# Latent attention: the maxima from bf16 parts in one matmul, over all steps, and the product one tile later

## What is computed

```
cq = x @ W_q                      # latent queries, 32 wide (4 copies on 128 partitions)
kh = maps[h].T @ keys             # keys of head h in the same 32 dimensions
tilt = keys . tilt[h]             # one number per key and head
s[k, q] = kh[:, k] . cq[:, q] + tilt[k]
p = exp(scale * (s - max_k s))    # scale = 1 / sqrt(128 + 32)
out[h] = (V.T @ p) / sum_k p      # V: 32 wide, the same for all heads
```

## Time and profile before

| what | value |
|---|---|
| median of 3 runs | 4385.51 us |
| the profiled execution | 4400.56 us |
| its span | 4398.8 us |
| granted clock, mean over the span | 0.90 |
| TensorE busy | 3628.2 us (82%) |
| VectorE busy | 3012.3 us (68%) |
| ScalarE busy | 2482.7 us (56%) |
| POOL busy | 1168.0 us (27%) |
| latent attention, head loop | 1095 to 1806 us of the span |

### The profile page before, as it was taken

How to read it: one execution, slowest core, us unless ns; L and a number is a source line. 1 busy time by engine, 2 the same in 40 slices (tenths; PEclk the granted TensorE clock), 3 DMA queues, 4 the chain that set the end, 5 groups by cost and what they waited for, 6 DMA issues and landing times. The chain is left out here.

```text
span 4398.8 us, 86825 instructions
## 1 busy us (share of the span) xinstructions
PE 3628.2 (82%) x33381; PEld 1655.7 (38%) x33381; DVE 3012.3 (68%) x4370; ACT 2482.7 (56%) x4824; POOL 1168.0 (27%) x1181
## 2 busy tenths in 40 slices
PE   5769998754888888687999997778995779999957
PEld 4523333633222222342222223355654612222237
DVE  6567774557565665658999994435994489999933
ACT  3436665463144444433888886434543548888844
POOL 2610000524465664000000000035883500000016
PEclk7879999876799999896999998878996879999979
DMA  3221110210000000002000000140001120000012
GB/s 122 70 78 38 40 42 15 83 32 9 2 4 5 7 4 5 18 0 71 27 25 31 31 21 3 27 116 14 1 1 63 57 76 25 31 31 23 20 54 73
DMA packets 82885, 153.20 MB, mean 35 GB/s; under 512 B 22940, under 2 KB 49196, under 8 KB 81580
## 3 DMA queue, kind: packets, MB, share of 16 engines
q1 hardware_dynamic: 56856, 105.74, 7.6%
q0 software_dynamic: 12704, 22.97, 1.8%
q10 hardware_dynamic: 12916, 18.93, 1.3%
HBM read 103.76 MB, written 31.20 MB: 31 GB/s over the span
## 5 line engine op out<-in xcount | busy, mean ns | idle before, releaser
L1516 DVE TENSOR_REDUCE 55_heads_mx<-55_heads_mps 128x1 f32<-128x1024 f32 x512 | 602.8, 1220 | 49.1 <-PE 55_heads_mps L1366 46.7
L1516 DVE TENSOR_REDUCE 32_heads_mx<-32_heads_mps 128x1 f32<-128x1024 f32 x512 | 602.7, 1220 | 47.5 <-PE 32_heads_mps L1366 45.1
L1486 ACT ACTIVATE 55_heads_p<-55_heads_sps 128x512 f32<-128x512 f32 x1024 | 553.7, 596 | 86.2 <-PE 55_heads_sps L1392 83.0
L1486 ACT ACTIVATE 32_heads_p<-32_heads_sps 128x512 f32<-128x512 f32 x1024 | 553.7, 596 | 85.9 <-PE 32_heads_sps L1392 82.5
L2581 ACT ACTIVATE 21_latent_heads_p<-21_latent_heads_ring 128x1024 f32<-128x1024 f32 x256 | 257.8, 1024 | 350.9 <-PE 21_latent_heads_ring L2486 348.5
L1516 DVE TENSOR_REDUCE 7_heads_mx<-7_heads_mps 128x1 f32<-128x1024 f32 (+7 forms) x384 | 333.8, 909 | 147.7 <-PE 7_heads_mps L1374 100.9
L1486 ACT ACTIVATE 7_heads_p<-7_heads_sps 128x512 f32<-128x512 f32 (+3 forms) x640 | 308.1, 533 | 156.2 <-PE 7_heads_sps L1395 116.5
L2610 DVE TENSOR_REDUCE 21_latent_heads_mx<-21_latent_heads_ring 128x1 f32<-128x1024 f32 x256 | 302.3, 1220 | 130.0 <-PE 21_latent_heads_ring L2465 130.0
L2395 POOL TENSOR_TENSOR 21_latent_heads_psum<-21_latent_heads_psum,21_latent_heads_p 128x1024 f32<-128x1024 f32 x140 | 328.4, 2349 | 85.8 <-ACT 21_latent_heads_p L2581 81.0
L1392 PE MATMUL 55_heads_sps<-51_head_rows_qs,51_head_rows_ks 123*32 123x512 bf16 x4096 | 314.3, 383 | 8.3 <-ACT 55_heads_p L1486 5.0
L1392 PE MATMUL 32_heads_sps<-30_head_rows_qs,30_head_rows_ks 123*32 123x512 bf16 x4096 | 314.1, 383 | 8.4 <-ACT 32_heads_p L1486 5.0
(11 more groups left out here) (1217 smaller groups left out, 6778.8 us busy)
## 6 DMA issues: line engine op xcount, KB each, us to landing
3_routed_experts<-in_L0f_experts SPq DMA_DIRECT2D x8, 514.0 KB
9_routed_experts<-in_L0f_experts SPq DMA_DIRECT2D x8, 514.0 KB, 6.5
50_routed_experts<-in_L3f_experts SPq DMA_DIRECT2D x8, 514.0 KB
57_routed_experts<-in_L3f_experts SPq DMA_DIRECT2D x8, 514.0 KB
38_hale_masks_qs<-scratch_q_parts SPq DMA_DIRECT2D x11, 288.0 KB
38_hale_masks_ks<-scratch_k_parts SPq DMA_DIRECT2D x33, 96.0 KB
yT<-scratch_results SPq DMA_DIRECT2D x12, 256.0 KB, 6.3
y<-scratch_results ACTq DMA_DIRECT2D x12, 256.0 KB, 6.6
```

What stands on the lines that cost most here:

```text
L1486: act.activation(pslot[x % PS][:, 0:CW - off], sps[e % SB][:, 0:CW - off], ACT.Exp, scale=SCALE / 2).then_inc(ex_done, 1)
L1516: dve.tensor_reduce(mx[h % 2][:, i, half:half + 1], mps[x % 2][:, 0:w], AX.X, ALU.max).then_inc(mx_taken, 1)
```

## The change

It does these things, all in the latent attention:

- The maxima are made from bf16 parts in a single matmul per bank: `rough_k` holds keys rounded to bf16 (96 rows), where the second 32 rows become the rest (keys minus rounded keys), and 3 rows of tilt; `rough_q` holds the rounded queries, where the third 32 rows become their rest, and 3 rows of ones. 99 rows are contracted: rounded times rounded, rest times rounded, rounded times rest, and tilt. Rounding is ScalarE's, the rest VectorE's (`rest_of_keys`), and keys are made two heads ahead.
- Maxima run six units ahead of the score passes, and one comes with each score pass, over all 32 passes of a head: `maxima_at`. Per key tile the order is two score passes, two maximum passes, then the product of the tile before.
- A score pass takes its row groups by its queries' chunk: the even pass of a tile uses rows 0 to 63, the odd one rows 64 to 127. The tilt is no longer in the side matmul; it is the bias of the exponential, a column of `tilt_bias`. The side matmul only subtracts the maximum (`minus`), and `q_side` is 512 wide, filled by 12 DMAs of 4 x 128 elements where it was 4 of 48 x 128.
- The denominators' matmuls move to pass 9 (5 in the last head), in the order column group by column group. ScalarE copies their result. The reciprocal is in four pieces, at passes 11 to 14.
- POOL adds passes 0 to 25, and in the last head the even ones up to 22; VectorE adds the rest, three passes late.

The core of the diff:

```diff
-    SUMS = 6
-    FIRST, LAST = 6, 24
-    TURNED = 28
-    MAKE = (FIRST - 1, FIRST + 1)
-    BY_DVE = tuple(range(24, S))
+    AHEAD = 6
+    SUMS = 9
+    MAKE = (17, 21)
+    TURNED = 29
+    LAG = 3
+    INVERT = (11, 12, 13, 14)
+    BY_DVE = tuple(range(26, S))
...
+        def maxima_at(h, p):
+
+            v = h * U + p + AHEAD
+            return [(1 + v // U, v % U)] if v < U * LASTH else []
...
                 for h in range(MLA_H):
                     sp.wait_ge(m_copied, h + 1)
-                    for top in range(0, P, DC):
-                        sp.dma_start(q_side[h % 2][top + 3:top + 6, :], mT[h % 2][0:PARTS, :]).then_inc(m_in[h % 2], 16)
+                    for c in range(NC):
+                        for a in range(3):
+                            at = a * NT + TPC * c
+                            sp.dma_start(q_side[h % 2][DC * c + a:DC * c + a + 1, :], mT[h % 2][at:at + TPC, :]).then_inc(m_in[h % 2], 16)
...
                     for x in range(2):
-                        r = rows(number, x)
-                        pe.matmul(bank(number, x), cq[r, tile(i)], kh[h % 2][r, chunk(2 * pair + x)], start=True, stop=False,
-                                  tile_position=(r.start, 0))
...
+                        ins = pe.matmul(bank(("max", h, u), x), rough_q[0:K_ROWS, tile(i)], rough_k[h % 2][0:K_ROWS, chunk(2 * pair + x)],
+                                        start=True, stop=True)
+                    ins.then_inc(mx_ready, 1)
...
                     for p in range(S):
-                        scores(p, h)
...
+                        scores(h, p)
+                        if p % 2:
+                            for unit in maxima_at(h, p - 1) + maxima_at(h, p):
+                                max_pair(*unit)
+                            if p > 1:
+                                product(h, p // 2 - 1)
+                            elif h:
+                                product(h - 1, NT - 1)
+                        if h + 2 < MLA_H and p in MAKE:
+                            make_keys(h + 2, MAKE.index(p))
+                        if h and p == sums_at(h):
                             denominators(h - 1)
...
+                        act.activation(slot(p, h)[:], pair_of(("score", h, p))[:], ACT.Exp, scale=MLA_SCALE,
+                                       bias=tilt_bias[:, h, p // 2:p // 2 + 1]).then_inc(ex_done, 1)
```

353 lines of the change are left out of this document (191 added, 162 removed).

## The result

The changed kernel takes 4422.0 us (median of 4 runs, 4418.17 to 4426.78), the kernel before 4385.2 (median of 4, one run more than the three shown ahead): a ratio of 1.0082, 95% interval 1.0066 to 1.0098. It is slower by 0.8%. The prediction was 4337 us, faster, with a range up to 4385: wrong in its sign and outside its range.

A forecast was written before the change was run, and what follows sets the result against it. TensorE and the chain through it were taken to set the pace. Head 0 -6.7, heads 1 to 6 -31.9, head 7 -15.1, start +4.4, end +0.5 gave -48.8 us from 4385.5: 4337 us, range 4285 to 4385.

The forecast's parts named there:

- Other engines fit under it: Main loop: VectorE's two reductions a tile and POOL's 55.9 us a head fit under the chain's 64.2 us a head.
- before head 0: Start of the head loop: fewer tilt DMAs save time, subtractions and twelve DMAs add it, +4.4 us together.
- head 7, to its last exponential's end: Last head: POOL takes even sums up to pass 22, a tile per 2.33 us; 43.3 us, was 58.4.
- tail: End of the last head: the reciprocal cut in pieces adds 0.5 us.
- The tile of 4.01: Main loop: scores, exponential with bias, release, second maximum and product chain to 4.01 us a key tile, 64.2 a head.
- The boundary: Between heads: TensorE waits for twelve SP issues and their landing, 5.5 us, 8.1 before the last head.
- Half clock behind the boundary: First tiles after a head's boundary stall: TensorE at half clock for 7 us of work, costing 2.6 us a head.
- Rival 3: Main loop: POOL's later start or slower additions make the tile longer than its chain; +28 us, 4365; chance 0.13.
- Rival 1: Between heads: issues of short pieces are far cheaper, so stall and half clock go; 52 us less, 4285; chance 0.14.
- Rival 2: First tiles of each head: half clock lasts 4.5 tiles, costing 11.0 us instead of 2.6; 4396; chance 0.12.
- Rival 4: Main loop: score passes no longer overlap or another ring wait makes a tile 4.4 us; +44, 4381; chance 0.05.
- The signs I had listed for "wrong": Heads under 72 or over 85 us apart, exponentials waiting for POOL, low clock over half a head, or the product waiting.

The follow-up runs named there:

- experiment 2: The changed kernel with the rows of maxima sent in four DMAs a head instead of twelve: 4379.53 us, ratio 0.9978 to the kernel before.
- experiment 3: The changed kernel with POOL's additions on 8 of 1024 columns, result not the network's: 4334.94 us, ratio 0.9886 to the kernel before.
- experiment 4: The changed kernel with two additions fewer a head on POOL (VectorE from pass 24 instead of 26): 4409.6 us, ratio 1.0059 to the kernel before.

## Why the prediction was wrong

**The step that failed** is the one sentence on the other engines: "Other engines fit under it: VectorE has two reductions a tile ..., POOL 24 additions a head, 2.33 each ..., 55.9." Both fit by busy time and neither fits beside the other. The sum took VectorE's other instructions at the durations they have while POOL pauses and had no term for VectorE waiting for POOL. It also compared POOL's 55.9 us with the whole head, 64.2, though POOL's share lies in passes 2 to 25, twelve tiles of 4.01, which are 48.1. At a turn of 4.11 us POOL needs 4.6 for its two additions, falls behind, and makes 12 or more additions without a pause before the multiplication comes. That made the multiplication 9.5 us, the stall behind it 5.74, and a second stretch at half clock. It cost 8 us in head 0, 9 to 13 in each of heads 1 to 6, and 4 to 7 us in and behind the last head. With most of POOL's work left out the kernel takes 4335.

**Head by head**, in the profiled executions:

| | forecast | after | from |
|---|---|---|---|
| before head 0 | +4.4 | +0.25 | first scores 1157.56, were 1157.31; 1.5 of it is the stages ahead, see below |
| head 0 | 78.8 | 87.1 | 1157.56 to 1244.70 |
| heads 1 to 6 | 466.8 | 531.0 | 1244.70 to 1775.72 |
| head 7, to its last exponential's end | 43.3 | 49.8 | to 1825.5 |
| tail | +0.5 | +4.5 | 11.1 to the last multiplication's end, was 6.6 |

These differences are 78.8 us too long together; the rest of the program, which varies by more than that between traces, was 4 us shorter, which leaves the 75 by which the span missed the forecast of -48.8 against its +26.2. By the medians the miss is 85 (4422 for 4337), since the profiled execution of the kernel before is 15 us above its median and that of the changed one 5.

**What held.** The tile of 4.01 was 4.11: the product starts 0.54 after the second maximum, where 0.43 was priced (1274.85 and 1275.39 in the rows above). The exponential with its bias column takes 1.11 against 1.02, as forecast. The boundary: 4.3 to 4.8 for 5.5, and 7.03 for 8.1 at head 7; here the rows on SP's issues were right against the Trainium skill's sentence on issues, which the prediction weighed, and experiment 2 shows the price: 43 us for eight issues a head and the clock behind them. Half clock behind the boundary was the 7 us I took, or more: the mean clock of 77 us in experiment 3, without any other stall, is 0.95, which is 8 us at half.

```profile
1240.00:1317.00 77.00, 60.38 (x405) 14.39 (x397) 50.20 (x50) 38.72 (x38) 4.84 (x24) 0.95 0.02 4
```

**What was off in size.** Before head 0 the copy of the maxima comes at 1148.65, 4 us earlier than before, where my terms came to -0.4 (one tilt DMA for four, -2.2, the two subtractions, +2.2, a faster pace, -0.4). 1.5 us of these 4 are not the change's: the stages ahead ended that much earlier in this trace (stage 19 starts at 1059.2, before at 1060.7). In experiment 4's trace, where this part of the kernel is the same, stage 19 starts at 1063.2 and the first scores come at 1161.55. Measured from there, the start grew by 1.8 us where +4.4 was forecast. Head 7: POOL's even and VectorE's odd additions take turns, 3.2 us each where 2.36 and 1.22 were priced.

**The rivals.** Rival 3 had the right engine, POOL, and the wrong way: it let POOL's additions be slow and its last be late, at 2 to 6 us a head. Their mean is 2.43 us against 2.35, and ScalarE waited 0.8 us in all for POOL's sums (and 6.1 for VectorE's). What was held up was the engine that shares with it, in the middle of a head. Rivals 1, 2 and 4 did not happen. The signs I had listed for "wrong" included heads apart by over 85 us, which is what came.

**What in the profile of before could have told.** The multiplication of head 0's result, 0.69 us, started at 1262.32, in the gap of 2.01 us between the end of POOL's run of three additions and the next one (the first two rows of POOL's timeline above), and POOL's rows there are parted by idle times of 0.2 to 3.7 us. The forecast pace removed those gaps by its own arithmetic: 64.2 us for 32 exponentials is 2.0 apiece, an addition 2.33. What that trace could not tell is what VectorE does when the gaps are gone; the forecast had a warning there, not a price.

## What to carry to other kernels

Before a change makes a loop faster, compare the new turn not only with each engine's busy time but with POOL's time for its share of a turn: once POOL falls behind and has no pause left, a VectorE instruction that takes two operands from SBUF or copies within it can wait for the end of POOL's whole run, and everything queued behind it on VectorE waits too. The remedy costs nothing if one operand can lie in PSUM, or if the instruction can stand where POOL is idle. And a wait removed moves to the next instruction of the kind: list them all (here a multiplication, a subtraction, a cast of 16 elements) before pricing the cure of the first.
